# Attention on one core: the product with the values split into two halves of 64 keys, beside the scores and the maxima

## The chip, the core and the metric

The kernel runs on one core of a Trainium2 chip. A core has five engines with a queue of instructions each: TensorE (PE, matrix products; its weight loads are listed apart as PEld), VectorE (DVE), ScalarE (ACT), GpSimd (POOL) and SyncE (SP, which issues DMA transfers here). They meet only through semaphores. TensorE multiplies a stationary operand (the weights, loaded first) with a moving one that streams through its array of 128 rows by 128 columns, and writes into PSUM, which has eight banks of 512 float32 columns. An instruction may use a tile of the array: 64 rows by 128 columns, 128 rows by 32 columns, and so on; rows go with the partitions of the operands, columns with the partitions of the output.

The metric is the time of one execution on the device in microseconds (us), lower is better. Beside it stands the profile of one execution, whose span is the time from its first to its last instruction.

## The reference, cut to what matters

```python
def _L0_attn_ref(x, w_q, s_q, b_q, w_k, s_k, b_k, w_v, s_v, b_v, w_o, s_o, b_o):   # x: 8 x 1024 x 256
    q = split_heads(_tlin(x, w_q, s_q, b_q))       # 16 heads of 16
    k = split_heads(_tlin(x, w_k, s_k, b_k))
    v = split_heads(_tlin(x, w_v, s_v, b_v))
    scores = jnp.einsum('bhqd,bhkd->bhqk', q, k) / jnp.sqrt(jnp.float32(HEAD))
    attn = jax.nn.softmax(scores, axis=-1)
    ctx = jnp.einsum('bhqk,bhkd->bhqd', attn, v)
    ctx = ctx.transpose(0, 2, 1, 3).reshape(B, S, H)
    return _tlin(ctx, w_o, s_o, b_o)
...
x = _layernorm(x + _L0_attn_ref(x, ...), axis=-1)
x = _layernorm(x + _L0_ffn_ref(x, ...), axis=-1)   # FP4-quantized gate, up (704) and down
```

## The kernel before

Three programs follow one another on every engine: `project` (queries, keys and values, 0 to about 201 us), `attend` (the attention, about 201 to 1476 us) and `feed` (output projection, layer norms, FFN). The change lies in the TensorE program of `attend` alone.

**Tiling of the attention.** There are 8 sequences of 16 heads. A group is four heads of one sequence, so there are 32 groups (`NGR`). A head's queries and keys are split into high and low parts that are stacked along the contraction: 48 rows for a maximum (`KR`), 50 for a score (`KM`, with two more rows that subtract the row's maximum). Two heads of a group lie in partitions 0 to 63, two in 64 to 127; `half` names this half of the array, `pair` the head within it. A group takes 16 steps (`ST`): 2 halves of 512 queries (`qh`) by 8 tiles of 128 keys (`kt`).

**A step** has three kinds of products:
- Scores: four tiles, one a head, of 128 keys by 512 queries (`score_tile`, L935, tile size 64x128), for the step that comes next. ScalarE takes each from one of three PSUM banks and writes its exponential to `prob` (`room` in the profile, L1025).
- Maxima: two units of 128 queries by 1024 keys, each two matmuls of 512 columns (`max_bank`, L913, tile size 64x128), for a group ahead. Unit u lies in half `u % 2`. VectorE reduces both banks of a unit in one instruction (L1079), and a unit's banks are free again two units later (`max_read`).
- Values: the exponentials of the step before times the values (`values`, L966): for each of the 4 heads 17 output columns (16 and the row's sum), each head in its own 32 columns of the array, all 128 keys in one contraction (tile size 128x32), the 512 queries as two halves of 256. It all accumulates in bank 7 (`PV`) over the 8 key tiles. A float32 matmul shows as two records in the trace, so a half of a step shows 8.

**Order on TensorE before.** Half a step is: a maximum's bank, a score tile, the other bank, another score tile, then the values of 256 queries (`max_and_scores`, then `values`). `SCORE_ORDER = (1, 3, 0, 2)` puts the scores into the half of the array that this half step's maxima don't use, so each maximum has a score beside it. There are 490 steps of this form (`BARE`), with 980 units of maxima; the last 22 have no maxima and are written apart.

**Waits.** A score tile waits until ScalarE has read the tile three before it (`prob_ready`); a unit of maxima waits for `max_read`; the values wait for all four exponentials of their step. SP and POOL carry stacks, maxima and results around and are not touched.

Of the kernel before, what the change touches and what calls it, by code (L numbers as in the profile page):

```python
# [17 lines left out]
BANK = 512  # L18
NB, S, H = 8, 1024, 256
T = NB * S  # L20
# [4 lines left out]
GH = 4  # L25
NG = NH // GH
AV = 32
GP = GH // 2
HALF = P // 2
# [3 lines left out]
DV = D + 1  # L33
NTILES = T // P
KR = SLOTS * D
KM = KR + 2
SCORE_ORDER = (1, 3, 0, 2)
ALONE_ORDER = (1, 0, 3, 2)
RING = 3
PR = 3  # L40
# [2 lines left out]
NGR = NB * NG  # L43
# [3 lines left out]
QH = S // BANK  # L47
# [67 lines left out]
def wait(eng, sem, n):  # L115

    if isinstance(n, int):
        if n > 0:
            eng.wait_ge(sem, n)
    else:  # L120
        assert n.min_val > 0
        eng.wait_ge(sem, n)
# [637 lines left out]
def attend(nc, sb, sem, room, qk_dram, vals, ctx_dram, rden_dram, ps, ident, ffn_ws, amax_w, rcp_w,  # L760
# [4 lines left out]
    KT = S // P  # L765
    ST = QH * KT
    SRING = 3
    MX, SC, PV = 0, 4, 7
# [3 lines left out]
    prob = room[:, :].rearrange("p (r h n) -> p r h n", r=PR, h=GH)  # L772
    wgu = sb("wgu", [WB, 2, 8, H])
    max_psum = sem("max_psum")
    max_read = sem("max_read")
    score_psum = sem("score_psum")
    prob_ready = sem("prob_ready")
    pv_done = sem("pv_done")
    fq_chain = sem("fq_chain")
    passing_in = sem("passing_in")  # L780
    passing_ready = sem("passing_ready")

    def projections_done(eng):

        for j in range(2):
# [5 lines left out]
    BARE = (NGR - 1) * ST - AHEAD  # L791
# [3 lines left out]
    FILL_PE = {(NGR - 1) * ST + 2: (1, 0), (NGR - 1) * ST + 3: (1, 1),  # L795
               (NGR - 1) * ST + 6: (2, 0), (NGR - 1) * ST + 7: (2, 1)}
    FILL_ACT = {(NGR - 1) * ST + 6: (1, 1), (NGR - 1) * ST + 8: (2, 2), (NGR - 1) * ST + 11: (2, 1)}

    def number(i, s):

        return i.k * ST + s

    def paired(i, s):


        return number(i, s) > BARE

    def score_order(i, s):


        return ALONE_ORDER if paired(i, s) else SCORE_ORDER

    def score_bank(i, s, n):

        if paired(i, s):
            return BARE_BANKS[((number(i, s) - BARE - 1) * GH + n) % len(BARE_BANKS)]
        return SC + (number(i, s) * GH + n) % SRING

    def prob_slot(i, s):

        return (i.k * ST + s) % PR

    def scores_due(i, s, n):

        return s * GH + n - (len(BARE_BANKS) if paired(i, s) else SRING) + 1
# [9 lines left out]
    def groups():  # L835

        return (At(None, k, RING) for k in range(-1, NGR))
# [64 lines left out]
    def tensor(pe):  # L902
# [15 lines left out]
        def score_tile(i, s, n):  # L918
            slot = i.slot(RING)
            if s == 0 and n == 0:  # L920

                pe.wait_ge(maxima_out.arrived, i.lin(ARRIVED, ARRIVED))

            wait(pe, prob_ready, i.lin(ST * GH, scores_due(i, s, n)))
            if number(i, s) == BARE + 1 and n == 0:

                pe.wait_ge(max_read, len(item))
            if i.k == 0 and s * GH + n < SRING:

                pe.wait_ge(qk_float, 4 * (T // BANK) - 1 + n % 2)  # L930
                pe.wait_ge(v_ready, 2 * (T // BANK) - 1)
            qh, kt = divmod(s, KT)
            pair, half = divmod(score_order(i, s)[n], 2)
            rows = slice(half * HALF, half * HALF + KM)
            nc.tensor.matmul(ps[:, score_bank(i, s, n), :],  # L935
                             ks[rows, slot, pair, kt * P:(kt + 1) * P],
                             qs[rows, slot, pair, qh * BANK:(qh + 1) * BANK],
                             start=True, stop=True).then_inc(score_psum, 1)

        def max_and_scores(j, u, ahead, first):  # L940

            if j is not None:
                max_due(j, u)
            for bank in range(QH):
                if j is not None:
                    last = max_bank(j, u, bank)
                    if bank == QH - 1:
                        last.then_inc(max_psum, 1)
                if ahead is not None:
                    score_tile(*ahead, first + bank)  # L950

        def values(i, s, half):

            qh, kt = divmod(s, KT)
            cols = slice(half * BANK // 2, (half + 1) * BANK // 2)
            if half == 0:
                pe.wait_ge(prob_ready, i.lin(ST * GH, (s + 1) * GH))
                if kt == 0:  # L960
                    wait(pe, craw_ready, i.lin(QH, qh))
                if i.k == 0 and s == 0:

                    pe.wait_ge(v_ready, 2 * (T // BANK))
            for h in range(GH):
                last = nc.tensor.matmul(ps[h * AV:h * AV + DV, PV, cols],  # L966
                                        vals[:, i.k // NG * KT + kt, i.k % NG * GH + h, :],
                                        prob[:, prob_slot(i, s), h, cols], start=kt == 0 and half == 0,
                                        stop=kt == KT - 1 and half == 1)
            if half == 1:  # L970
                last.then_inc(pv_done, 1)

        def weights_across(n):


            u, piece = divmod(n, PIECES)
            if not 0 <= u < 2 * HC:
                return
            m, c = divmod(u, HC)
            if n == 0:  # L980
                pe.wait_ge(fq_chain, FQ_STEPS)
            if piece == 0:
                wait(pe, wt_split, u)
            for j in range(4 * piece, 4 * piece + 4):
                last = nc.tensor.transpose(ps[:, WT + j // 4, (j % 4) * WB:(j % 4 + 1) * WB],
                                           wgu[:, m, j, c * P:(c + 1) * P], ident[0:WB, 0:WB])
            if piece == PIECES - 1:
                last.then_inc(wt_psum, 1)

        piece = [0]  # L990
        for i in groups():
            for s in range(ST - 1 if i.k < 0 else 0, ST):
                ahead = (i.plus(1), 0) if s == ST - 1 else (i, s + 1)
                ahead = ahead if ahead[0].ok(NGR) else None
                j, u = maxima(i, s)
                j = j if j.ok(NGR) and i.k >= 0 else None
                max_and_scores(j, u, ahead, 0)
                before = (i, s - 1) if s else (i.plus(-1), ST - 1)
                if number(i, s) >= BARE:

                    max_and_scores(None, None, ahead, 2)
                    for half in range(2):
                        values(*before, half)
                    if number(i, s) in FILL_PE:
                        k, c = FILL_PE[number(i, s)]
                        fill.tensor(pe, [k], [c])
                    else:
                        weights_across(piece[0])
                        piece[0] += 1
                    continue  # L1010
                if before[0].ok(NGR):
                    values(*before, 0)
                max_and_scores(j, u + 1, ahead, 2)
                if before[0].ok(NGR):
                    values(*before, 1)
        for half in range(2):
            values(At(None, NGR - 1, RING), ST - 1, half)

# [630 lines left out]
```

## Time and profile before

| | us |
|---|---|
| median of 3 runs | 2023.29 (2022.61 to 2023.70) |
| the profiled execution's own time | 2024.02 |
| its span, first to last instruction | 2022.2 |
| TensorE busy / VectorE busy / ScalarE busy in that span | 1983.0 / 1859.8 / 1680.1 |
| mean granted TensorE clock | 0.995 of full speed |

Busy time counts an instruction from its start to its end, and instructions on TensorE overlap: a row of the timeline with x8 and 0.63 is eight instructions whose first start and last end are 0.63 us apart. An instruction that waits inside the array for its weights, or for the array to be empty, counts as busy too or leaves a gap that is covered by the modelled end of the one before. So for TensorE the distance from start to start tells more than its busy share.

### The profile page before, as it was taken

Reading aid. Unit: us, or ns where it says so; the run is one execution under the profiler, and the core shown is the slowest. Engines: PE = TensorE matmul, PEld = TensorE weight load, DVE = VectorE, ACT = ScalarE, POOL = GpSimd, SP = SyncE. Lnnn points to the kernel's source line nnn. Section 1 sums busy time; section 2 is a strip of 40 time slices with the busy share of each in tenths; the row PEclk is TensorE's granted clock in tenths of the full one; section 3 lists DMA queues with packets and bytes.
Section 4 is the critical chain, followed back from the end, with each engine's and each line's share of the span. In section 5 each row is a group of like instructions: output and inputs, shape, how many; then the busy total and the mean of one; then the engine's idle time right before and its main releaser. Section 6 shows DMA issues by size and latency. Waiting matters only on the chain.

```text
span 2022.2 us, 42087 instructions
## 1 busy us (share of the span) xinstructions
PE 1983.0 (98%) x15806; PEld 1039.8 (51%) x15806; DVE 1859.8 (92%) x2345; ACT 1680.1 (83%) x3244; POOL 753.0 (37%) x749
## 2 busy tenths in 40 slices
PE   8999999999999999999999999999999999999997
PEld 7766333333333333333333333333468888888876
DVE  4788899999999999999999999999479999999997
ACT  6655788888888898898888888888977777777776
POOL 3000364567566344001000100100136666666785
PEclk9999899999999999999999999999999999999999
DMA  7885443345434443533454354434111111111210
GB/s 226 283 243 203 91 75 56 60 84 104 87 75 94 94 92 75 102 89 84 87 101 91 71 98 90 92 79 108 44 38 46 55 53 48 48 48 53 63 32 27
DMA packets 119000, 181.40 MB, mean 90 GB/s; under 512 B 29644, under 2 KB 74444, under 8 KB 118796
## 3 DMA queue, kind: packets, MB, share of 16 engines
q1 hardware_dynamic: 111116, 171.10, 36.6%
q10 hardware_dynamic: 7392, 7.34, 1.1%
q8 instruction: 125, 2.05, 0.5%
q14 instruction: 79, 0.65, 0.1%
q0 software_dynamic: 288, 0.27, 0.1%
HBM read 103.68 MB, written 73.40 MB: 88 GB/s over the span
## 4 chain that ended last, share of the span: by engine, by line
PE 88%; DVE 5%; ACT 3%; issue 2%; DMA 1%; POOL 0%; SPq 0%; DVEq 0%; POOLq 0%; ACTq 0%
PE ps L913 30%; PE ps L966 28%; PE ps L1302 10%; PE ps L1341 5%; PE ps L494 4%; PE ps L504 3%; PE ps L1290 2%; ACT craw L1033 2%; PE ps L935 2%; PE ps L1313 2%; PE ps L481 1%; PE ps L1349 1%; DVE room L1490 1%; PE ps L1358 1%; DVE room L1568 1%
## 5 line engine op out<-in xcount | busy, mean ns | idle before, releaser
L1079 DVE TENSOR_REDUCE negmax<-ps 128x1 f32<-128x1024 f32 x980 | 1182.7, 1219 | 26.6 <-PE ps L913 21.2
L1025 ACT ACTIVATE room<-ps 128x512 f32<-128x512 f32 x2048 | 1102.8, 599 | 124.0 <-PE ps L935 92.7
L935 PE MATMUL ps<-qs,ks 50*128 50x512 f32 x2048 | 749.0, 450 | 1.9 <-ACT room L1025 1.0
L913 PE MATMUL ps<-ks,qs 48*128 48x512 f32 x1960 | 718.4, 446 | 0.0
L966 PE MATMUL ps<-room,vals 128*17 128x256 f32 x8192 | 639.7, 386 | 8.9
L913 PEld LDWEIGHTS ps<-ks,qs 48*128 48x128 f32 x1960 | 290.2, 185 | 417.5 <-DVE negmax L1079 330.0
L164 POOL CAST mrow<-turned_rows 128x32 fp32r<-128x32 f32 x32 | 6.7, 210 | 913.7 <-DVE turned_rows L159 699.5
L966 PEld LDWEIGHTS ps<-room,vals 128*17 128x17 f32 x8192 | 140.0, 95 | 372.6 <-issue 212.1
L935 PEld LDWEIGHTS ps<-qs,ks 50*128 50x128 f32 x2048 | 305.7, 185 | 17.8 <-ACT room L1025 13.6
L1302 PE MATMUL ps<-wguT,xqT 128*128 128x512 f32 (+1 forms) x1152 | 267.0, 385 | 3.9 <-DVE xqT L1530 3.9
L1302 PEld LDWEIGHTS ps<-wguT,xqT 128*128 128x128 f32 x1152 | 210.8, 188 | 51.6 <-issue 9.9
L1341 PE MATMUL ps<-wdT,hT 128*128 128x256 f32 x640 | 149.2, 380 | 1.8 <-ACT hT L1410 1.8
L1136 POOL TENSOR_SCALAR fq<-fq 88x1024 f32<-88x1024 f32 (+1 forms) x42 | 137.5, 3274 | 3.6
L1341 PEld LDWEIGHTS ps<-wdT,hT 128*128 128x128 f32 x640 | 115.2, 190 | 17.2 <-issue 2.4
L1608 POOL TENSOR_TENSOR hg<-room,hm 128x704 f32<-128x704 f32 x64 | 97.8, 1528 | 58.2 <-DVE room L1497 57.4
L569 ACT ACTIVATE qf<-ps,b_col,s_all 128x512 f32<-128x512 f32 x64 | 49.9, 780 | 53.5 <-PE ps L494 50.6
L1613 POOL TENSOR_TENSOR hq<-hg,blocks 128x704 f32<-128x704 f32 x64 | 88.8, 1388 | 5.0
L1418 ACT ACTIVATE bend_of_x<-fq 128x256 f32<-128x256 f32 x64 | 26.7, 418 | 75.4 <-DVE fq L1490 75.4
L1580 POOL TENSOR_TENSOR rstd<-rstd,numbers 128x1 f32<-128x1 f32 x128 | 82.7, 646 | 10.0
L1579 POOL TENSOR_TENSOR rstd<-mv,numbers 128x1 f32<-128x1 f32 x128 | 30.1, 235 | 151.2 <-DVE mv L1548 146.7
L494 PE MATMUL ps<-qs,wqk 128*128 128x512 f32 x256 | 80.9, 438 | 0.0
L1138 POOL TENSOR_TENSOR fq<-fq 88x1024 f32<-88x1024 f32 (+1 forms) x36 | 77.4, 2149 | 2.6
(111 smaller groups left out, 2131.6 us busy)
## 6 DMA issues: line engine op xcount, KB each, us to landing
qk_parts<-parts SPq DMA_DIRECT2D x64, 512.0 KB, 3.9
qs<-qk_parts SPq DMA_DIRECT2D x192, 128.0 KB, 4.4
ks<-qk_parts SPq DMA_DIRECT2D x192, 128.0 KB, 7.1
ctx_raw<-craw SPq DMA_DIRECT2D x64, 256.0 KB
ready<-passing SPq DMA_DIRECT2D x27, 512.0 KB, 6.7
pairs<-ready SPq DMA_DIRECT2D x27, 512.0 KB
out_dram<-fin SPq DMA_DIRECT2D x64, 128.0 KB, 1.7
xin<-in_L_attn_x_dram ACTq DMA_DIRECT2D x14, 512.0 KB, 5.7
```

What stands on the lines that cost most here:

```text
L494: last = nc.tensor.matmul(ps[:, QK + m % 2, :], wqk[:, a, m // 2, c, (m % 2) * P:(m % 2 + 1) * P], x_half[:, i.slot(2), c, :], start=n == ...
L913: return nc.tensor.matmul(ps[:, MX + 2 * (item[i.k, u] % 2) + bank, :], qs[rows, i.slot(RING), pair, t * P:(t + 1) * P], ks[rows, i.slot(R ...
L935: nc.tensor.matmul(ps[:, score_bank(i, s, n), :], ks[rows, slot, pair, kt * P:(kt + 1) * P], qs[rows, slot, pair, qh * BANK:(qh + 1) * BAN ...
L966: last = nc.tensor.matmul(ps[h * AV:h * AV + DV, PV, cols], vals[:, i.k // NG * KT + kt, i.k % NG * GH + h, :], prob[:, prob_slot(i, s), h ...
L1025: nc.scalar.activation(prob[:, prob_slot(i, s), score_order(i, s)[n], :], ps[:, score_bank(i, s, n), :], ACT.Exp, scale=float(D) ** -0.5). ...
L1079: nc.vector.tensor_reduce(negmax[:, j.slot(RING), max_column(u):max_column(u) + 1], ps[:, bank:bank + 2, :], AX.XY, ALU.max, negate=True). ...
L1136: link(nc.gpsimd.tensor_scalar(dst, norm, mid * mid, gain, ALU.is_gt, ALU.mult))
L1302: last = nc.tensor.matmul(ps[:, GU + n0 // BANK, 0:n1 - n0], xqT[:, a, c, :], wguT[:, b, c, n0:n1], start=n == 0 and c == 0, stop=n == len ...
L1341: last = nc.tensor.matmul(ps[:, DN[t.slot(2)], 0:H], hT[:, c, :], wdT[:, c, :], start=c == 4, stop=False)
L1580: nc.gpsimd.tensor_tensor(rstd[:, n, 1:2], rstd[:, n, 0:1], numbers[:, 1:2], ALU.pow).then_inc(sems[name], 1)
L1608: nc.gpsimd.tensor_tensor(hg[:, :], hn[:, t.slot(2)], hm[:, t.slot(2)], ALU.subtract).then_inc(sems["hgrid_ready"], 1)
L1613: nc.gpsimd.tensor_tensor(hq[:, :].rearrange("p (n e) -> p n e", e=BLK), hg[:, :].rearrange("p (n e) -> p n e", e=BLK), hs[:, t.slot(2), 1 ...
```

## The change

The values' product of a step is cut along the keys into two contractions of 64, one in each half of the array (tile size 64x32), and each is put beside the scores and the maxima of the half step that lie in the other half. `SCORE_ORDER` becomes `(0, 2, 1, 3)`, so that scores and maxima of a half step now share one half of the array. A half step is then: score tile, values of 64 keys for 256 queries, score tile, values of the same 64 keys for the other 256 queries, both banks of the unit of maxima. A new semaphore `high_keys_done` and the old `pv_done` keep the two halves of keys, which accumulate in the same bank, from running at once. The last 22 steps keep `values` as it was.

```diff
-SCORE_ORDER = (1, 3, 0, 2)
+SCORE_ORDER = (0, 2, 1, 3)
...
+        def half_step(half, j, u, ahead, before):
+            for cols in range(2):
+                if ahead is not None:
+                    score_tile(*ahead, 2 * half + cols)
+                if before is not None:
+                    values_of_half(*before, 1 - half, cols)
             if j is not None:
                 max_due(j, u)
-            for bank in range(QH):
-                if j is not None:
+                for bank in range(QH):
                     last = max_bank(j, u, bank)
-                    if bank == QH - 1:
-                        last.then_inc(max_psum, 1)
-                if ahead is not None:
-                    score_tile(*ahead, first + bank)
+                last.then_inc(max_psum, 1)
+
+        def values_of_half(i, s, keys, cols):
+            qh, kt = divmod(s, KT)
+            opens, closes = keys == 1 and cols == 0, keys == 0 and cols == 1
+            if cols == 0:
+                if keys == 1:
+                    wait(pe, pv_done, i.lin(ST, s))
+                else:
+                    pe.wait_ge(high_keys_done, i.lin(ST, s + 1))
+            if opens:
+                pe.wait_ge(prob_ready, i.lin(ST * GH, (s + 1) * GH))
+                if kt == 0:
+                    wait(pe, craw_ready, i.lin(QH, qh))
...
+            rows = slice(keys * HALF, (keys + 1) * HALF)
+            queries = slice(cols * BANK // 2, (cols + 1) * BANK // 2)
+            for h in range(GH):
+                last = nc.tensor.matmul(ps[h * AV:h * AV + DV, PV, queries],
+                                        vals[rows, i.k // NG * KT + kt, i.k % NG * GH + h, :],
+                                        prob[rows, prob_slot(i, s), h, queries], start=kt == 0 and opens,
+                                        stop=kt == KT - 1 and closes)
+            if cols == 1:
+                last.then_inc(high_keys_done if keys == 1 else pv_done, 1)
...
-                max_and_scores(j, u, ahead, 0)
                 before = (i, s - 1) if s else (i.plus(-1), ST - 1)
...
+                before = before if before[0].ok(NGR) else None
+                if number(i, s) < BARE:
+                    half_step(0, j, u, ahead, before)
+                    half_step(1, j, u + 1, ahead, before)
                     continue
-                if before[0].ok(NGR):
-                    values(*before, 0)
-                max_and_scores(j, u + 1, ahead, 2)
-                if before[0].ok(NGR):
-                    values(*before, 1)
```

TensorE, one whole step in the middle of the attention, before (L913 maxima, L935 scores, L966 values; a row of values is one instruction a head):

```order
L913 MATMUL ps<-ks,qs 128x512 [waits max_read]
L935 MATMUL ps<-qs,ks 128x512 [waits prob_ready]
L913 MATMUL ps<-ks,qs 128x512
L935 MATMUL ps<-qs,ks 128x512 [waits prob_ready]
L966 MATMUL ps<-room,vals 17x256 [waits prob_ready]
L966 MATMUL ps<-room,vals 17x256 x3
L913 MATMUL ps<-ks,qs 128x512 [waits max_read]
L935 MATMUL ps<-qs,ks 128x512 [waits prob_ready]
L913 MATMUL ps<-ks,qs 128x512
L935 MATMUL ps<-qs,ks 128x512 [waits prob_ready]
L966 MATMUL ps<-room,vals 17x256 x4
```

Now TensorE in a step of the same kind, after (L914 maxima, L936 scores, L983 values of 64 keys); the second unit of maxima, two rows like the first, follows the last row:

```order
L936 MATMUL ps<-qs,ks 128x512 [waits prob_ready]
L983 MATMUL ps<-room,vals 17x256 [waits prob_ready,pv_done]
L983 MATMUL ps<-room,vals 17x256 x3
L936 MATMUL ps<-qs,ks 128x512 [waits prob_ready]
L983 MATMUL ps<-room,vals 17x256 x4
L914 MATMUL ps<-ks,qs 128x512 [waits max_read]
L914 MATMUL ps<-ks,qs 128x512
L936 MATMUL ps<-qs,ks 128x512 [waits prob_ready]
L983 MATMUL ps<-room,vals 17x256 [waits high_keys_done]
L983 MATMUL ps<-room,vals 17x256 x3
L936 MATMUL ps<-qs,ks 128x512 [waits prob_ready]
L983 MATMUL ps<-room,vals 17x256 x4
```

Instructions of tile size 64x128 and instructions for the values now alternate more often: in a half step of before they change twice (maxima and scores, values), in one of after four times (score, values, score, values, then maxima that the next score follows). The number of value instructions doubles, each with as many columns as before.

## Rows read from the trace of the kernel before

**Rows 1.** The page: span, and busy time (share) and instructions by engine.

```profile
span 2022.2 us, 42087 instructions
...
PE 1983.0 (98%) x15806; PEld 1039.8 (51%) x15806; DVE 1859.8 (92%) x2345; ACT 1680.1 (83%) x3244; POOL 753.0 (37%) x749
```

**Rows 2.** Stretches: us, busy of PE, PEld, DVE, ACT, POOL (x), granted clock, DMA share, GB/s.

```profile
210.00:214.00 4.00, 4.00 (x26) 1.16 (x24) 2.45 (x2) 2.19 (x4) 0.00 (x0) 0.50 1.09 131
...
263.00:1400.00 1137.00, 1128.64 (x11022) 407.89 (x11020) 1119.76 (x976) 1019.62 (x1894) 350.86 (x242) 1.00 0.43 86
```

**Rows 3.** Chain that ended last, 800 to 806 us: shares, then pieces by start and length.

```profile
by line: PE ps L913 58.5%; PE ps L966 46.3%; PE ps L935 0.7%
...
801.28 0.56 PE ps L966 x8
```

**Rows 4.** Costliest groups: busy and mean ns, then idle before and releaser.

```profile
L1079 DVE TENSOR_REDUCE negmax<-ps 128x1 f32<-128x1024 f32 x980 | 1182.7, 1219 | 26.6 <-PE ps L913 21.2
...
L966 PE MATMUL ps<-room,vals 128*17 128x256 f32 x8192 | 639.7, 386 | 8.9
```

**Rows 5.** Timeline of VectorE, steady stretch, then the reduces behind a reciprocal.

```profile
243.93 6.10 DVE L1079 TENSOR_REDUCE negmax<-ps 128x1 f32<-128x1024 f32 x5
...
260.00 0.54 DVE L704 RECIPROCAL sums<-sums 64x64 f32<-64x64 f32 x1
260.46 5.71 DVE L1079 TENSOR_REDUCE negmax<-ps 128x1 f32<-128x1024 f32 x5
```

**Rows 6.** Timeline of ScalarE, one step's four exponentials; the same every 2.44 us.

```profile
304.40 2.25 ACT L1025 ACTIVATE room<-ps 128x512 f32<-128x512 f32 x4 [0.19 <-PE ps L935]
```

**Rows 7.** Timeline of TensorE's matmuls, 801.1 to 802.7 us: start, length, instruction.

```profile
801.21 0.63 PE L966 MATMUL ps<-room,vals 128*17 128x256 f32 x8
801.76 0.50 PE L913 MATMUL ps<-ks,qs 48*128 48x512 f32 x1
801.77 0.50 PE L935 MATMUL ps<-qs,ks 50*128 50x512 f32 x1
802.10 0.39 PE L913 MATMUL ps<-ks,qs 48*128 48x512 f32 x1
...
802.43 0.62 PE L966 MATMUL ps<-room,vals 128*17 128x256 f32 x8
```

**Rows 8.** Timeline of TensorE's weight loads, same stretch; in brackets idle before, releaser.

```profile
801.20 0.13 PEld L966 LDWEIGHTS ps<-room,vals 128*17 128x17 f32 x8 [0.37 <-issue]
801.76 0.18 PEld L913 LDWEIGHTS ps<-ks,qs 48*128 48x128 f32 x1 [0.42 <-DVE negmax L1079]
...
801.87 0.19 PEld L913 LDWEIGHTS ps<-ks,qs 48*128 48x128 f32 x1
...
802.42 0.13 PEld L966 LDWEIGHTS ps<-room,vals 128*17 128x17 f32 x8 [0.37 <-ACT room L1025]
```

**Rows 9.** Projection stage: sizes 128x128 throughout, type changes; matmuls, one load row.

```profile
50.67 0.40 PE L494 MATMUL ps<-qs,wqk 128*128 128x512 f32 x1
50.90 0.62 PE L494 MATMUL ps<-xl,wqk 128*128 128x512 f32 x2
...
51.13 0.64 PEld L504 LDWEIGHTS ps<-wT,xT 128*128 128x128 f32 x3
```

**Rows 10.** Projection stage: maxima of size 64x128 (L481), then size 128x128 (L504); matmuls, one load row.

```profile
135.74 0.49 PE L481 MATMUL ps<-ks,qs 48*128 48x512 f32 x2
136.17 0.92 PE L504 MATMUL ps<-wT,xT 128*128 128x256 f32 x3
...
136.16 0.73 PEld L504 LDWEIGHTS ps<-wT,xT 128*128 128x128 f32 x4 [0.24 <-issue]
```

**Rows 11.** Timeline of TensorE's matmuls at the lower clock.

```profile
209.38 0.79 PE L913 MATMUL ps<-ks,qs 48*128 48x512 f32 x1
...
210.53 1.06 PE L966 MATMUL ps<-room,vals 128*17 128x256 f32 x8
211.52 0.79 PE L913 MATMUL ps<-ks,qs 48*128 48x512 f32 x1
```

More of the change, by code:

```diff
@@ L778, in attend @@
     pv_done = sem("pv_done")
+    high_keys_done = sem("high_keys_done")
     fq_chain = sem("fq_chain")
@@ L938, in score_tile, with scores @@
                              start=True, stop=True).then_inc(score_psum, 1)
-        def max_and_scores(j, u, ahead, first):
+        def scores(ahead, first):
+            if ahead is not None:
+                for n in (first, first + 1):
+                    score_tile(*ahead, n)
+        def half_step(half, j, u, ahead, before):
+            for cols in range(2):
+                if ahead is not None:
+                    score_tile(*ahead, 2 * half + cols)
+                if before is not None:
+                    values_of_half(*before, 1 - half, cols)
             if j is not None:
                 max_due(j, u)
-            for bank in range(QH):
-                if j is not None:
+                for bank in range(QH):
                     last = max_bank(j, u, bank)
-                    if bank == QH - 1:
-                        last.then_inc(max_psum, 1)
-                if ahead is not None:
-                    score_tile(*ahead, first + bank)
+                last.then_inc(max_psum, 1)
[11 more added lines that the diff above has]
+                    wait(pe, craw_ready, i.lin(QH, qh))
+                if i.k == 0 and s == 0:
+                    pe.wait_ge(v_ready, 2 * (T // BANK))
+            rows = slice(keys * HALF, (keys + 1) * HALF)
[7 more added lines that the diff above has]
+                last.then_inc(high_keys_done if keys == 1 else pv_done, 1)
         def values(i, s, half):
@@ L996, in tensor @@
                 j = j if j.ok(NGR) and i.k >= 0 else None
-                max_and_scores(j, u, ahead, 0)
                 before = (i, s - 1) if s else (i.plus(-1), ST - 1)
[L999 to L1009, printed above, removed]
-                    continue
-                if before[0].ok(NGR):
-                    values(*before, 0)
-                max_and_scores(j, u + 1, ahead, 2)
-                if before[0].ok(NGR):
-                    values(*before, 1)
+                before = before if before[0].ok(NGR) else None
+                if number(i, s) < BARE:
+                    half_step(0, j, u, ahead, before)
+                    half_step(1, j, u + 1, ahead, before)
+                    continue
+                scores(ahead, 0)
+                scores(ahead, 2)
+                for half in range(2):
+                    values(*before, half)
+                if number(i, s) in FILL_PE:
+                    k, c = FILL_PE[number(i, s)]
+                    fill.tensor(pe, [k], [c])
+                else:
+                    weights_across(piece[0])
+                    piece[0] += 1
         for half in range(2):
```

## The prediction

> **What bounds the kernel now.** I read the busy shares first. TensorE is busy 98% of the span, VectorE 92%, ScalarE 83% [rows 1]. In the attention, 263 to 1400 us, it is 1128.64, 1119.76 and 1019.62 of 1137 us, at a granted clock of 1.00, that is 2.4 GHz [rows 2]. Three engines look nearly full, so shares alone don't say which sets the pace. The chain of what ended last does: between 800 and 806 us it never leaves TensorE; it alternates between maxima and values [rows 3].
>
> The second witness is VectorE. Its 980 reduces are 1.22 us apart in a steady stretch (five in 6.10, (6.10 - 1.22) / 4) [rows 4, 5], with hardly any idle time, as if it set the pace. But behind a reciprocal, when a unit of maxima already waits for it, it does five in 5.71 us, so start to start is (5.71 - 1.22) / 4 = 1.12 us [rows 5]. In the steady stretch it could go faster and isn't fed faster. ScalarE's four exponentials of a step take 2.25 of 2.44 us and are followed by an idle 0.19 for a score [rows 6], so it could follow down to 1.12 us a half step. TensorE bounds the attention at 1.22 us per half step, 980 half steps of the form that the change touches, and the next two limits lie at 1.12.
>
> Third, what those 1.22 us are [rows 7, 8]. Two pairs (a maximum and a score that start 0.01 apart, in different halves of the array) and the values of 256 queries. From the pairs' first weight load to the values' first load it is 802.42 - 801.76 = **0.66**; from the values' load to the next pair's 801.76 - 801.20 = **0.56**. Sum 1.22. Inside the 0.66 the second pair's weights are loaded at 801.87, while the first pair is in flight: within one tile size, loads run ahead. Between tile sizes they don't. The values' loads stand at 802.42, though the second pair started at 802.10 and 512 columns need only about 0.23, the distance of the matmuls of 512 columns at 50.67 and 50.90 [rows 9]. So about 0.1 us passes with nothing new in the array. The same on the way back: the second set of four value matmuls starts about 0.63 - 0.39 = 0.24 behind the first [rows 4, 7], at 801.45, lasts another 0.23, and the next load stands at 801.76, 0.08 to 0.1 later. The releasers named in brackets there, VectorE and "issue", are not the cause: nothing starts early in any half step, whoever was done long before.
>
> Is it the tile size or the data type that costs it? The pairs are float32r, the values float32. The projection answers. From L494 to L504 the type changes in the same way but both are 128x128, and the first load of L504 starts at 51.13, just as the last L494 matmul (0.23 behind 50.90) starts: it runs ahead, no gap [rows 9]. From L481, 64x128, to L504, 128x128, the load starts 136.16 - 135.74 = 0.42 behind that of L481, though the two L481 matmuls run together: about 0.11 for their own weights (801.76 to 801.87), 0.21 for the columns, 0.1 of nothing [rows 8, 10]. The gap goes with the size of the tile. In every such place of this trace both sizes use common rows of the array. Whether it also comes when they lie in separate halves, as they will here, no row shows, and everything hangs on that.
>
> **The change part by part.**
>
> Columns streamed: none removed. Each half of the array has per step 2 scores, 2 banks of maxima and, before, 2 halves of values; after, the values' 4 sets run with 64 keys instead of 128, twice as many instructions of equal length, each set in one half only. The sum per half of the array is the same. So the change gains only by removing the gaps, or by packing them beside other work, and it moves twice as many size changes into each half step: 4 for 2.
>
> If a change of size empties the whole array, no value matmul runs beside a score, and a half step is a row of phases: maxima and the next half step's first score, then values, score, values. The first is like the two pairs of before: two matmuls in turn in one half, the score beside the second in the other: 0.66 [rows 8]. A phase of values is 0.56, whether 64 or 128 rows deep, since length goes by columns: I take this from the same rows; were 64 rows quicker to empty than 128, it could save no more than the 0.1 of nothing. A single score stands like the single L481 pair: 0.42 [rows 10]. Sum 0.66 + 0.56 + 0.42 + 0.56 = **2.20**, against 1.22. That is 0.98 more, 980 times: +960 us.
>
> Waits: `high_keys_done` and `pv_done` hold TensorE's own queue, and behind them stand a score and the maxima. In this case the values' last set is over a whole phase (0.66) before the next values need it, so they cost nothing. `prob_ready` is for exponentials two half steps old, and a half step of 2.20 leaves ScalarE (1.12) and VectorE (1.12) waiting for TensorE, not the other way. A score's bank is freed early for the same reason. Moving the maxima to the end of the half step hides behind nothing and delays nothing: VectorE then has 2.20 us for a reduce of 1.12. SP, POOL and the last 22 steps keep their work and order. The copy of the finished values (every 16th half step) lies in the 0.66 of the scores and maxima as before. All cost zero here, and each would come back if the phases ran side by side.
>
> The Trainium skill, "TensorEngine Tiling (Array Packing)", Key Properties, says that changing the tiling mode, and not just the tile, drains the TensorE, and lists 64x128 and 64x32 as different modes. The gaps at 802.42 and 136.16 agree; the case of separate halves no run here shows yet. By that rule the time would be the 2.20 us above. The same page says that tiles operate independently, which alone would give the faster rival below.
>
> **The sum.** The profiled execution took 2024.0 us, 0.7 over the median. 2024 + 960 = **2984 us**. Its own range: each of the four boundaries may be 0.03 us cheaper or dearer, 4 x 0.03 x 980 = 118, so 2880 to 3090.
>
> **The rivals.**
>
> *Side by side (faster).* The tiles of the two halves know nothing of each other. Then the chain is: a set of values starts, sets two to four follow at 0.23 each (0.69), the first bank of maxima starts in queue order with the fourth, the second 0.23 later (0.92), its columns end 0.22 later, and only then can the values of the next half step use that half: 1.14 to 1.15 us. Gain 0.07 x 980 = 69 us: 1955. VectorE and ScalarE stop it at 1.12 us, so not under about 1925; if the values' own semaphores, which now have only some 0.2 us of room, bind, up to 2010. For it: pairs of one size in separate halves do start 0.01 apart [rows 7]. Against it: the load that never runs ahead into another size.
>
> *A gap, but only in the half that changes.* Same chain with 0.1 before the values may enter: 1.24 us, 0.02 x 980 = +20 us: 2044, range 2010 to 2080. The 0.1 on the other change, values to score, hides behind the maxima of the other half. For it: all rows read so far are consistent with it too, since all share rows. It decides to the slower side as soon as the gap is over 0.08.
>
> *Part of the phases overlap.* The load waits for the drain of the other half but the streams of scores and values still overlap: between 1.24 and 2.20, say 2500.
>
> *The clock.* Near 210 us the granted clock is 0.50 (1.2 GHz), behind a stretch where TensorE had waited between its first score tiles, and a half step takes 211.52 - 209.38 = 2.14 us [rows 2, 11]. This also confirms who sets the pace. Were the array's thinner use to keep the clock there, each phase goes up by 2.14 / 1.22 = 1.75: 3.86 us a half step, about 4600 us.
>
> **How the numbers follow.** The whole array empties: 0.60. Side by side: 0.21. Gap in one half only: 0.11, of which 0.03 lands within 0.2%. Partial overlap: 0.05. Clock: 0.03. The gap that is seen at each change of size and never at a change of type or tile makes the first likeliest; that no row has the two sizes in separate halves keeps the others. Range: to hold 8 in 10 it has to reach from the faster rival to the top of the likeliest: 1930 to 3090; only the low clock and an end of each case stay out. Faster by over 0.2% (what a measurement of this kernel can tell from no change): 0.21; within: 0.03; slower: 0.76.
>
> **What would show it.** Right: VectorE's reduces 2.2 us apart; each row of values begins over 0.4 us behind its score, and each score about 0.56 behind a row of values; VectorE's busy share near 60%. Wrong: a score (L936) starting while value matmuls (L983) of the other half stream, loads of 17 columns issued within 0.1 us of a score's start, reduces 1.15 to 1.24 us apart. Then the step that failed is the one from gaps in common rows to gaps in separate halves.

## The result, and the profile after

| | us |
|---|---|
| before, median of 4 runs | 2022.95 |
| after, median of 4 runs | 4554.91 (4550.61 to 4556.86) |
| ratio, with its 95% interval | 2.2521 (2.2482 to 2.256) |
| the profiled execution's own time / span | 4554.67 / 4552.9 |
| mean granted TensorE clock | 0.587 |

The change makes the kernel slower by 2532 us. The forecast was 2984, its range ended at 3090, and the time lies far outside. It lies where the last of the rivals stood, the one with the clock, which was given 3 chances in 100.

From the page of the changed kernel, busy time by engine, the granted clock in 40 slices, and the costliest groups; they answer to [rows 1, 4]:

```profile
PE 4522.3 (99%) x23630; PEld 1662.4 (37%) x23630; DVE 1881.8 (41%) x2345; ACT 1792.0 (39%) x3244; POOL 748.9 (16%) x749
...
PEclk9955555555555555555555555555555555699999
...
L1114 DVE TENSOR_REDUCE negmax<-ps 128x1 f32<-128x1024 f32 x980 | 1200.1, 1225 | 2530.5 <-PE ps L914 2530.5
...
L983 PE MATMUL ps<-room,vals 64*17 64x256 f32 x15648 | 2054.3, 616 | 0.0
```

VectorE has the same 980 reduces and nearly the same busy time (1200.1 us for 1182.7), and now waits 2530.5 us for maxima instead of 26.6: nearly the whole loss stands in one row, and all of that waiting is for TensorE's maxima. The clock row says the rest: the attention runs at 1.2 GHz from its start to its end, slices 3 to 34.

The timeline of TensorE's matmuls, 2000 to 2008 us, in the steady state; it answers to [rows 7, 11]:

```profile
2001.01 0.79 PE L914 MATMUL ps<-ks,qs 48*128 48x512 f32 x1
2001.01 0.79 PE L936 MATMUL ps<-qs,ks 50*128 50x512 f32 x1
2001.60 0.62 PE L914 MATMUL ps<-ks,qs 48*128 48x512 f32 x1
2002.15 1.05 PE L983 MATMUL ps<-room,vals 64*17 64x256 f32 x8
2003.13 0.79 PE L936 MATMUL ps<-qs,ks 50*128 50x512 f32 x1
2003.85 1.05 PE L983 MATMUL ps<-room,vals 64*17 64x256 f32 x8
2004.83 0.79 PE L914 MATMUL ps<-ks,qs 48*128 48x512 f32 x1
```

These are the four phases of the prediction, one behind the other: maxima with a score 1.14 us, values 0.98, score 0.72, values 0.98, together 3.82 us from 2001.01 to 2004.83. Nothing of the values runs beside a score. (The score starts with the first bank of maxima, though it is queued behind the second; it gains nothing, since the phase lasts until the second bank is through.) 980 half steps times 3.82 - 1.22 = 2.60 us is 2548 us, and 2532 were measured.

Where the clock goes: stretches of the changed kernel, columns as in [rows 2], the eighth number being the granted clock.

```profile
200.00:203.00 3.00, 3.00 (x14) 1.94 (x12) 2.81 (x4) 1.71 (x3) 0.00 (x0) 1.00 0.50 188
203.00:206.00 3.00, 2.55 (x10) 1.28 (x9) 1.04 (x4) 2.40 (x5) 0.00 (x0) 1.00 0.59 221
206.00:210.00 4.00, 4.00 (x25) 1.52 (x24) 2.36 (x2) 2.72 (x6) 0.00 (x0) 0.67 0.81 131
...
400.00:3900.00 3500.00, 3500.00 (x18291) 987.61 (x18291) 1135.41 (x971) 1120.23 (x1886) 347.37 (x242) 0.50 0.14 28
```

It falls at the start of the attention, within 4 us of a wait of 0.45 us for ScalarE between the first score tiles. The kernel before loses it at the same place, and has it back by 222 us:

```profile
206.00:210.00 4.00, 4.00 (x26) 1.31 (x24) 2.46 (x3) 2.05 (x4) 0.00 (x0) 0.50 1.10 135
222.00:230.00 8.00, 8.00 (x80) 2.88 (x76) 7.64 (x7) 6.53 (x13) 0.00 (x0) 1.00 0.68 156
```

So two questions were open. Does a change of tile size really empty the half of the array that isn't concerned, or do the order and the new waits keep scores and values apart? And what holds the clock at 0.50: the number of changes, the rows that stand idle, or the low state in which the attention starts?

### The profile page after: what moved, and what is told of

The parts are those of the page before. It is cut to its first block, busy times and chain, and to the rows that moved or that the text cites. A ratio compares the mean times of both kernels' runs of the same rounds, so it can differ in the third digit from the quotient of the medians.

```text
span 4552.9 us, 58162 instructions
## 1 busy us (share of the span) xinstructions
PE 4522.3 (99%) x23630; PEld 1662.4 (37%) x23630; DVE 1881.8 (41%) x2345; ACT 1792.0 (39%) x3244; POOL 748.9 (16%) x749
## 4 chain that ended last, share of the span: by engine, by line
PE 96%; DVE 2%; issue 1%; DMA 0%; ACT 0%; POOL 0%; SPq 0%; DVEq 0%; POOLq 0%; ACTq 0%
PE ps L983 42%; PE ps L914 24%; PE ps L936 16%; PE ps L1337 4%; PE ps L1376 2%; PE ps L494 2%; PE ps L504 1%; PE ps L1325 1%; PE ps L1348 1%; PE ps L1004 0%; PE ps L481 0%; PE ps L1384 0%; DVE room L1525 0%; PE ps L1393 0%; DVE room L1603 0%
## 5 line engine op out<-in xcount | busy, mean ns | idle before, releaser
L1114 DVE TENSOR_REDUCE negmax<-ps 128x1 f32<-128x1024 f32 x980 | 1200.1, 1225 | 2530.5 <-PE ps L914 2530.5
L1060 ACT ACTIVATE room<-ps 128x512 f32<-128x512 f32 x2048 | 1214.7, 598 | 2426.7 <-PE ps L936 2418.8
L983 PE MATMUL ps<-room,vals 64*17 64x256 f32 x15648 | 2054.3, 616 | 0.0
L936 PE MATMUL ps<-qs,ks 50*128 50x512 f32 x2048 | 1571.0, 776 | 2.5 <-DVE negmax L1114 1.4
L914 PE MATMUL ps<-ks,qs 48*128 48x512 f32 x1960 | 1190.8, 707 | 0.0
L936 PEld LDWEIGHTS ps<-qs,ks 50*128 50x128 f32 x2048 | 567.1, 280 | 829.4 <-ACT room L1060 819.5
L914 PEld LDWEIGHTS ps<-ks,qs 48*128 48x128 f32 x1960 | 487.4, 308 | 813.5 <-issue 813.4
L983 PEld LDWEIGHTS ps<-room,vals 64*17 64x17 f32 x15648 | 291.6, 107 | 1060.1 <-issue 1059.9
L1068 ACT ACTIVATE craw<-ps 128x512 f32<-128x512 f32 x64 | 38.2, 597 | 127.2 <-PE ps L983 127.1
L504 PE MATMUL ps<-wT,xT 128*128 128x256 f32 x256 | 69.9, 396 | 0.0
```

The costliest lines, as they stand in the source:

```text
L504: last = nc.tensor.matmul(ps[:, VV + j // 2, (j % 2) * H:(j % 2 + 1) * H], xT[:, i.slot(2), c, j * P:(j + 1) * P], wT[:, 0, c, :], start=c ...
L914: return nc.tensor.matmul(ps[:, MX + 2 * (item[i.k, u] % 2) + bank, :], qs[rows, i.slot(RING), pair, t * P:(t + 1) * P], ks[rows, i.slot(R ...
L936: nc.tensor.matmul(ps[:, score_bank(i, s, n), :], ks[rows, slot, pair, kt * P:(kt + 1) * P], qs[rows, slot, pair, qh * BANK:(qh + 1) * BAN ...
L983: last = nc.tensor.matmul(ps[h * AV:h * AV + DV, PV, queries], vals[rows, i.k // NG * KT + kt, i.k % NG * GH + h, :], prob[rows, prob_slot ...
L1060: nc.scalar.activation(prob[:, prob_slot(i, s), score_order(i, s)[n], :], ps[:, score_bank(i, s, n), :], ACT.Exp, scale=float(D) ** -0.5). ...
L1114: nc.vector.tensor_reduce(negmax[:, j.slot(RING), max_column(u):max_column(u) + 1], ps[:, bank:bank + 2, :], AX.XY, ALU.max, negate=True). ...
```

## Experiment 1: one tile size for all

```diff
-            for h in range(GH):
-                last = nc.tensor.matmul(ps[h * AV:h * AV + DV, PV, queries],
-                                        vals[rows, i.k // NG * KT + kt, i.k % NG * GH + h, :],
-                                        prob[rows, prob_slot(i, s), h, queries], ...
+            last = nc.tensor.matmul(ps[:, PV, queries],
+                                    vals[rows, i.k // NG * KT + kt].rearrange("p h d -> p (h d)")[:, 0:P],
+                                    prob[rows, prob_slot(i, s), 0, queries], ...
```

> The changed kernel with the four value products of a set (tile size 64x32 each) replaced by one product of tile size 64x128 on the first head's exponentials; the other heads' values are left out and the output isn't the reference's. Columns streamed per half of the array and the order are those of the changed kernel: a set of four at once takes 0.23 us there, one 256-column float32 record 0.215. Theory A (a change of tile size empties the whole array): no change of size is left, score and values run side by side, half step 1.15 us, no less than VectorE's 1.12, so 1925 to 1990 us, and the clock stays at 1.00. Theory B (the order and the new waits on the values' own semaphores cost it, not the size): the phases stay apart, about 0.42 us from a score to its values at full clock, and the time stays near the changed kernel's, 2984 us at full clock or 4555 at half.

Measured 2007.12 us at a mean clock of 0.999 (before, on the same chip: 2021.95). TensorE's weight loads and matmuls, 1001.7 to 1003 us:

```profile
1001.76 0.18 PEld L982 LDWEIGHTS ps<-room,vals 64*128 64x128 f32 x1 [0.24 <-PE ps L982]
...
1001.76 0.48 PE L982 MATMUL ps<-room,vals 64*128 64x256 f32 x1
1001.78 0.48 PE L936 MATMUL ps<-qs,ks 50*128 50x512 f32 x1
1002.09 0.38 PE L982 MATMUL ps<-room,vals 64*128 64x256 f32 x1
1002.17 0.50 PE L914 MATMUL ps<-ks,qs 48*128 48x512 f32 x1
1002.30 0.38 PE L982 MATMUL ps<-room,vals 64*128 64x256 f32 x1
1002.50 0.39 PE L914 MATMUL ps<-ks,qs 48*128 48x512 f32 x1
```

A value product and a score start 0.02 us apart, and values and maxima interleave. The half step is 1.19 us here (1001.76 to 1002.95 for the next such pair), a little over the 1.15 expected, and the time lies over the 1925 to 1990 expected: the load at 1001.76 waits 0.24 us for the values of the other half of keys (`high_keys_done` and `pv_done` in turn), whose room had been put at 0.2 us. In the mean from 300 to 1400 us the reduces are 1.23 us apart (1.24 in the kernel before): about 0.6 us every 16 half steps goes to the copy of the finished values. The order and the waits are those of the changed kernel, and the phases are gone. Theory B falls.

The start of the attention shows something more. This run has the same wait of 0.45 us between its first score tiles, at 202.32 us, and its clock doesn't fall:

```profile
203.00:206.00 3.00, 3.00 (x17) 2.15 (x16) 1.71 (x2) 3.00 (x8) 0.00 (x0) 1.00 0.49 137
206.00:210.00 4.00, 4.00 (x30) 2.97 (x27) 4.00 (x5) 3.89 (x9) 0.00 (x0) 1.00 1.06 134
```

So the wait alone doesn't cost the clock; what TensorE does behind it counts too.

## Experiment 2: the same with only the size changed back

```diff
-            for h in range(GH):
+            for h in range(1):
```

(in both functions of the values, with the tile size 64x32 of the changed kernel)

> The changed kernel with the first head's value products alone (one of tile size 64x32 instead of four); the other heads' values are left out and the output isn't the reference's. It is the run with one product of size 64x128 with nothing but the tile size changed back. Theory A (the change of size empties the array): phases of the changed kernel stay, 2.2 us a half step at full clock and 3.8 at half: about 4500 us, the clock at 0.50. Theory B2 (it was the number of instructions or the four heads' streams at once that kept score and values apart): they run side by side as there, about 2007 us.

Measured 4519.75 us, clock 0.587. Its matmuls:

```profile
1000.16 0.79 PE L936 MATMUL ps<-qs,ks 50*128 50x512 f32 x1
1000.88 1.03 PE L983 MATMUL ps<-room,vals 64*17 64x256 f32 x2
1001.84 0.79 PE L914 MATMUL ps<-ks,qs 48*128 48x512 f32 x1
```

The phases are back with a quarter of the value instructions, 0.72 us from a score to values and 0.96 back. Between this run and the first one lies the width of the value product, and with it the tile size (the last 22 steps, which also have one product here and four there, carry no maxima); 64x32 beside 64x128 in separate halves doesn't run at once. The two runs don't part the width of the weights from the tile size, but the gap of [rows 10] stands between two products that are both 128 columns wide.

## Experiments 3 to 5: which part brings the clock down

The order of the scores alone, put into the kernel before:

```diff
-SCORE_ORDER = (1, 3, 0, 2)
+SCORE_ORDER = (0, 2, 1, 3)
```

> The kernel before with the order of scores (0, 2, 1, 3) alone: maxima and scores of a half step share one half of the array, the values keep 128 rows, two changes of size a half step as before. Phases: 0.11 for the weights, 4 x 0.23, 0.1 to empty, then 0.56 for values: 1.69 us a half step if the clock holds, 2024 + 0.47 x 980 = 2485 us. Theory G (the clock falls because of the many changes of size and their gaps): as many changes as before, clock 1.00, 2485. Theory H (the clock falls because half of the array's rows stand idle in many phases): here the other half is idle for 1.1 of 1.69 us, clock 0.50, half step 1.69 x 1.75 = 2.95, about 3720 us.

The kernel before, its values in four parts of 128 queries, one behind each pair (`values(*before, n)` with `cols = slice(n * BANK // 4, (n + 1) * BANK // 4)`):

> The kernel before, with the values of a step in four parts of 128 queries and one part behind each pair of maximum and score: four changes of size a half step, as in the changed kernel, but all rows of the array used by every phase. A pair alone 0.42 us, values of 128 queries 0.02 + 2 x 0.11 + 0.1 = 0.34: half step 1.52 us, 2024 + 0.30 x 980 = 2318 us at full clock. Theory G (clock falls by the number of changes): clock 0.50, 1.52 x 1.75 = 2.66, about 3430 us. Theory H (clock falls by idle rows): clock 1.00, 2318.

The changed kernel, with its phases put together:

```diff
+            scores(ahead, 2 * half)
             for cols in range(2):
-                if ahead is not None:
-                    score_tile(*ahead, 2 * half + cols)
                 if before is not None:
                     values_of_half(*before, 1 - half, cols)
```

> The changed kernel with both scores of a half step first, then the values of 64 keys for all queries, then the maxima: two changes of size a half step instead of four, same products. Maxima of one half and the next scores in the other run together: 0.66 us; values 4 x 0.23 + 0.1 = 1.02. Half step 1.68 us, 2475 us at full clock. Theory A: the two phases that went save 0.52 us of 2.20. Theory G: with as few changes as before the clock stays 1.00: 2475. Theory H: rows 0 to 63 or 64 to 127 stand idle for 1.02 of 1.68 us, clock 0.50, 2.94 a half step, about 3700 us.

Measured: 3724.07, 3321.88 and 3728.95 us, clocks 0.607, 0.619 and 0.607 (one execution each, as in all experiments but 10 and the first of 8 and 9). All three are at 0.50 from 206 us until the maxima end (3122, 2718 and 3126 us); a stretch of each, in this order:

```profile
800.00:840.00 40.00, 40.00 (x160) 17.73 (x159) 16.04 (x14) 16.33 (x28) 7.12 (x7) 0.50 0.09 28
...
400.00:1600.00 1200.00, 1197.42 (x9340) 410.01 (x9332) 579.64 (x496) 568.58 (x963) 284.19 (x167) 0.50 0.20 40
...
800.00:840.00 40.00, 40.00 (x274) 13.01 (x266) 16.68 (x15) 15.24 (x29) 3.11 (x6) 0.50 0.13 41
```

The first and the third came within 30 us of what theory H said; the second went as theory G said, 108 us under its 3430. So neither theory holds alone: few changes with idle rows lose the clock, and so do many changes with all rows used. The first line of the diff, alone, is worth 1700 us. All of them need longer than 1.22 us for the products of a half step, but that alone isn't it either: the kernel of experiment 10, at 1.34 us, loses the clock at the same place and is back at 1.00 from 214 us on. So the question was turned round: is it the form of the work or the state in which it starts?

## Experiments 6 and 7: several forms in one kernel

The half step takes its form from its group, `FORMS[max(0, i.k) // 4]`; `SCORE_ORDER` goes with it and the count for `high_keys_done` counts only the steps that use it.

> Whole attention computed, in stretches of four groups (128 half steps) that take turns: form of before; form of after; before; after's four changes and 64-key values but each score back beside a maximum (phases 0.42 + 0.56 + 0.42 + 0.56 = 1.96 us); before; values in two parts of 128 queries in every second half step alone (1.52 and 1.22, mean 1.37); before; after with its two scores together and its value phases together (1.68). Theory S (the clock falls in the thin start of the attention, where the kernel before loses it too, and the changed form only can't bring it back): the first stretch brings it back to 1.00 as before, and a stretch that is entered at 1.00 stays there: 2.20 us a half step in the second. Theory T (the changed form itself brings it down wherever it stands, and the form of before brings it back): granted clock 0.50 in the second stretch from a few us behind its start, 3.83 us a half step; 1.00 again in each stretch of before. For the fourth and the sixth stretch T has no forecast but the rank: the more phases with little in them, the sooner it falls; the sixth shows how far the kernel before stands from losing the clock. Times: S about 2024 + 128 x (0.98 + 0.74 + 0.15) + 84 x 0.46 = 2302 us; T with all four at 0.50 about 2024 + 128 x (2.61 + 2.21 + 1.18) + 84 x 1.72 = 2936 us.

> As the kernel with stretches before it, in the order: form of before; values in four parts of 128 queries (1.52 us a half step at full clock, all rows used); before; order of scores alone (1.69); before; one change pair a step (both half steps' maxima and scores, then all values: 0.11 + 8 streams in two halves 4 x 0.23 + 0.1 = 1.13, then 1.02: 2.15 a step, 1.08 a half step, but VectorE's 1.12 and the ring of three score banks hold it to 1.12 to 1.25); form of after; before. Theory T (the form of a stretch sets the clock): 0.50 in the second, fourth and seventh, 1.00 in the others. Theory S (only the start of the attention brings it down): 1.00 in all but the first 20 us.

Measured: 2699.79 us (clock 0.822; theory S said 2302, theory T 2936) and 2464.36 us (0.899). From the first kernel, stretches: the end of the first form of before; the changed form, which starts at 360.33 us; from 849 us before's form again; the form with paired scores, which starts at 1013 us; and the grouped form:

```profile
340.00:360.00 20.00, 19.86 (x188) 7.53 (x188) 19.00 (x18) 17.27 (x33) 12.58 (x7) 1.00 0.06 17
363.00:366.00 3.00, 2.85 (x30) 0.92 (x29) 1.97 (x2) 1.98 (x4) 2.92 (x1) 1.00 0.00 0
366.00:370.00 4.00, 4.00 (x21) 1.17 (x21) 1.70 (x2) 1.39 (x3) 3.91 (x2) 0.51 0.91 192
...
849.00:864.00 15.00, 15.00 (x88) 4.58 (x84) 8.91 (x9) 8.25 (x17) 0.00 (x0) 0.50 0.73 112
864.00:880.00 16.00, 15.85 (x156) 5.85 (x148) 15.72 (x14) 13.72 (x26) 0.00 (x0) 0.99 0.22 63
...
1018.00:1022.00 4.00, 4.00 (x28) 0.95 (x28) 1.23 (x1) 1.94 (x4) 3.77 (x4) 0.50 0.58 156
...
1980.00:2080.00 100.00, 99.42 (x1208) 39.62 (x1200) 74.65 (x65) 67.22 (x125) 6.23 (x10) 1.00 0.29 71
```

Entered at 1.00, the changed form has lost the clock about 6 us behind its start, and before's form brings it back in about 15. The form with paired scores (fourth stretch) has lost it about 5 us behind its start, and the changed form in the second kernel, which starts at 1267.06, has lost it by 1274. Just ahead of each of these falls the values start late, behind the copy of the finished ones (at 1017.95 TensorE idles 0.38 us for it), so whether the form would lose the clock without that short wait no run shows. The wait alone doesn't do it: the values in four parts have the same 0.38 us, at 412.98 in the second kernel, and keep 1.00. So does the grouped form, last row above, and the order of scores alone in the second kernel:

```profile
400.00:540.00 140.00, 137.73 (x1780) 56.70 (x1778) 109.89 (x95) 108.24 (x185) 72.21 (x34) 1.00 0.36 69
740.00:920.00 180.00, 180.00 (x1287) 86.35 (x1288) 133.28 (x115) 121.23 (x222) 46.69 (x36) 1.00 0.32 65
```

These are the same three forms that stood at 0.50 when the whole attention had them. At full clock their half steps fit the sums: for the four parts 90 reduces start between 399.5 and 539.8 us, 1.58 us apart (forecast 1.52); with the order alone 108 between 739.2 and 918.6, 1.68 apart (forecast 1.69). So theory T holds for the two forms with four changes and 64-key values, theory S for the others; the second kernel's T forecast (0.50 in three stretches) was right for one of them, its S forecast (1.00 in all) for all but that one.

The few microseconds of the changed form at full clock show what the forecast had been about. Matmuls from the first of the two kernels (L941 scores, L919 maxima, L1016 values):

```profile
361.32 0.49 PE L941 MATMUL ps<-qs,ks 50*128 50x512 f32 x1
361.74 0.62 PE L1016 MATMUL ps<-room,vals 64*17 64x256 f32 x8
362.29 0.49 PE L919 MATMUL ps<-ks,qs 48*128 48x512 f32 x1
...
362.95 0.62 PE L1016 MATMUL ps<-room,vals 64*17 64x256 f32 x8
363.50 0.50 PE L941 MATMUL ps<-qs,ks 50*128 50x512 f32 x1
```

Score to values 0.42, values 0.55, maxima with a score 0.66, values 0.55: 2.18 us from score to score, against the 2.20 of the sum.

## Experiments 8 and 9: the state at entry

The values in four parts as in experiment 4, with the first group alone in before's form (`FORMS = ['plain'] + ['quarters'] * 31`):

> The kernel with the values in four parts (3322 us when the whole attention has that form, at a granted clock of 0.50) with the first group alone, 20 half steps of maxima, in the form of before. Theory S2 (a form like this one can keep the clock but not bring it back; what decides is the state in which it is entered): the first group brings the clock to 1.00, it stays, half step 1.55 us as in the stretch of the earlier run, 2020 + 0.33 x 950 = 2333 us. Theory T2 (the stretch of that run was too short to lose the clock, a long one does): near 3300 us.

> Whole attention computed, stretches of four groups: form of before; form of after (takes the clock to 0.50); values in four parts, entered at the low clock; before; after; order of scores alone, entered at the low clock; before; values in two parts in every second half step. Theory S2: the third and the sixth stretch, which stood at 1.00 when they were entered at 1.00, now stay at 0.50, half steps 2.66 and 2.95 us; each stretch of before brings 1.00 back within some 20 us. Theory U (the form alone decides, the state at entry doesn't): they come back to 1.00 within 20 us, 1.55 and 1.68 us a half step. Times: S2 about 2024 + 128 x (2.61 + 1.44 + 2.61 + 1.73 + 0.15) = 3117 us; U about 2024 + 128 x (2.61 + 0.33 + 2.61 + 0.46 + 0.15) = 2812 us.

Measured: the first 2337.06 us (2333.32 to 2341.25), ratio to before 1.1566 (1.1542 to 1.1591), where the same form throughout had taken 3321.88 (with the values of the last 22 steps in four parts too, here in two). Its clock, by stretches:

```profile
204.00:208.00 4.00, 4.00 (x25) 1.14 (x23) 2.64 (x3) 2.62 (x6) 0.00 (x0) 0.51 1.07 185
...
216.00:220.00 4.00, 4.00 (x44) 1.41 (x44) 4.00 (x5) 3.49 (x7) 0.00 (x0) 1.00 0.96 197
...
400.00:1600.00 1200.00, 1182.01 (x15250) 487.07 (x15250) 944.14 (x811) 927.81 (x1574) 278.63 (x204) 1.00 0.36 71
```

One group of 32 decides 985 us. The second kernel shows the other direction; it took 3090.21 us (S2: 3117, U: 2812). Values in four parts and the order alone (first and last row), each entered at 0.50 behind a stretch of the changed form, and between them before's form, which starts behind the four parts at 1183 us and has the clock back 6 us later:

```profile
900.00:1180.00 280.00, 279.39 (x2184) 95.65 (x2180) 135.10 (x116) 132.88 (x225) 84.61 (x52) 0.50 0.20 42
1189.00:1193.00 4.00, 4.00 (x44) 1.29 (x36) 3.58 (x4) 3.27 (x8) 0.00 (x0) 0.95 0.95 186
...
1840.00:2200.00 360.00, 360.00 (x1444) 157.66 (x1444) 149.29 (x129) 147.26 (x248) 12.35 (x20) 0.50 0.20 38
```

Both stay low for their whole 330 and 380 us. Theory S2 holds: the values in four parts kept the clock for 1200 us in the first of these kernels, and didn't regain it in the 1200 us of experiment 4 shown above.

## Experiment 10: fewer changes instead of more

```diff
-                if before[0].ok(NGR):
-                    values(*before, 0)
                 max_and_scores(j, u + 1, ahead, 2)
                 if before[0].ok(NGR):
+                    values(*before, 0)
                     values(*before, 1)
```

> The kernel before with the values of both query halves behind the second half step's maxima and scores: one pair of size changes a step instead of two, same products. If each change costs its 0.1 us and the 0.11 of exposed weights, a step is 1.13 + 1.02 = 2.15 us against 2.44; VectorE allows 2.24, which gives 2024 - 0.2 x 490 = 1926 us at best. Rival: there are only three banks for scores, the fourth score of the burst waits for the first one's exponential (about 0.17 + 0.06 + 0.6 us behind its end), some 0.3 us, and nothing is left: 2000 to 2050 us.

Measured 2144.42 us, ratio 1.0608 (1.0588 to 1.0628), clock 0.996. Its matmuls and exponentials in one step:

```profile
1002.58 0.50 PE L913 MATMUL ps<-ks,qs 48*128 48x512 f32 x1
...
1002.93 0.67 PE L935 MATMUL ps<-qs,ks 50*128 50x512 f32 x2
1003.16 0.67 PE L913 MATMUL ps<-ks,qs 48*128 48x512 f32 x2
1003.83 0.50 PE L935 MATMUL ps<-qs,ks 50*128 50x512 f32 x1
1004.27 1.06 PE L966 MATMUL ps<-room,vals 128*17 128x256 f32 x16
1005.25 0.49 PE L913 MATMUL ps<-ks,qs 48*128 48x512 f32 x1
...
1003.18 2.06 ACT L1024 ACTIVATE room<-ps 128x512 f32<-128x512 f32 x4 [0.60 <-PE ps L935]
```

The values are as cheap as expected, 0.98 us in one piece. But the fourth score starts at 1003.83, 1.25 us behind the first pair, where its columns would allow 0.8: it waits for the bank of the first, whose exponential starts at 1003.18. And ScalarE then idles 0.60 us a step, from 1005.24 on: the next step's first score starts only when the values are through. A step is 2.67 us (1002.58 to 1005.25), where the rival's 2050 us would need 2.49. Here saving a change of size isn't worth the price of a burst that three banks can't hold. No version that was tried and that computes the whole attention beats the kernel before.

## Why the prediction was wrong, point by point

*Who sets the pace* ([rows 2 to 8]): right. TensorE at 1.22 us, VectorE and ScalarE could go faster; with one tile size the steady half step was 1.19.

*The gap goes with the tile size*: right, and so was the step from common rows to separate halves that everything was said to hang on. Experiments 1 and 2 differ in the width of the value product and show it both ways. The case "gap in one half only" and the faster rival are out; by experiment 1 independent tiles would have given about 2007 us rather than 1955, since the values' own semaphores bind (the rival's own bound for that was 2010).

*The sum of the phases*: right to 0.02 us. Forecast 0.66 + 0.56 + 0.42 + 0.56 = 2.20, measured 0.66 + 0.55 + 0.42 + 0.55 = 2.18 in the few microseconds at full clock.

*The 4 x 0.03 us of its own range, and the clock under it*: here it failed. The sum took every price at 2.4 GHz, and the range asked only how far a gap may vary. The term that was missing is a factor on all phases: 3.82 / 2.18 = 1.75, or 1.64 us x 980 = 1607 us. The rival for the clock had the consequence and the size (3.86 us and 4600 us, measured 3.82 and 4555): the new form keeps TensorE at 0.50. Its reason, the thinner use of the array, isn't shown: the values in four parts use all rows and stayed low too. Its evidence stood in [rows 2]: the kernel before has 0.50 at 210 us. I read that row as a blip of the start. It should have been read as a question: the clock can be lost in this stage, so does the new form keep it, and if it is lost, does it come back? For the changed form both answers are no: it lost the clock about 6 us after it was entered at 1.00, and never regained it. So the low start doesn't explain its time; it explains the 3322 us of the values in four parts. The start isn't the same for every version either, since the one of experiment 1 kept 1.00 through it. The sum itself makes the same products last 1.8 times as long, with half of the rows idle in three of four phases; no row showed that such a form keeps the clock or regains it, and the rival deserved far more than 3 in 100.

*The waits*: right in the sum, TensorE is busy 3500.00 of 3500 us and none of them shows. At full clock the copy of the finished values, put at nothing, would have shown a little, once in 16 half steps (the values at 365.37 us in experiment 6, where their phase would have begun at 365.15). Experiment 1 shows that they would have bound otherwise (0.24 us).

The Trainium skill, "TensorEngine Tiling (Array Packing)", Key Properties, has the drain on a change of mode, and the runs agree, also for tiles in separate halves. The Trainium skill, "TensorE: Matmul & The Clock Gate", section "HAM oscillation — how this bites in real kernels", tells how waits between bursts of matmuls cost the clock. Here the clock stayed down with TensorE busy 3500.00 of 3500 us in the profile, so a row that says busy is no promise of 1.00.

## What to carry to other kernels

Before instructions of different tile sizes are interleaved to fill idle parts of the array, look for one place in the trace where the size changes: if the next weight load stands behind the end of the old work, as it did here, each change costs a gap (0.1 us at full clock) and the parts won't run side by side. Then price the new form at both clock levels, and look at how the kernel enters the stage. Some forms kept the full clock but didn't regain it once it was lost; for the values in four parts, one group in the form of before ahead of them was cheap against that (2337 us for 3322). The changed form lost the clock from either start, so for it no such group would have helped for longer than a few microseconds.

## What was not expected of the hardware

- The clock's level depends on what went before: values in four parts ran at 1.00 for 1200 us when entered at 1.00 (1.57 us a half step) and at 0.50 for the 280 us shown when entered at 0.50 (2.57 us).
- The order of scores alone gives a half step of 1.68 us at 1.00, against 1.22 before, and of 2.99 at 0.50 (121 reduces that start between 1841.6 and 2200.0).
- A score queued behind two maxima of the other half started with the first of them (2001.01), ahead of the second (2001.60): both maxima need the same half of the array, the score the free one, and all three have one tile size.
- What exactly the chip looks at when it grants the clock stays open; idle rows with two changes of size, and four changes with all rows in use, each stayed at 0.50 after the fall at the start of the attention, and each kept 1.00 when it was entered there. The version with one tile size had the same wait at the start and no fall.
